# A vision tower on one core: first half's tokens in two column groups stored as plain rows, second half's stores cut by quarters, class value's products behind the first turnings

## The reference

```python
# 1. tokens: a state space kernel, 256 channels (two halves of 128), 64 complex states, 512 positions
dA = (1.0 + dtA / 2) / (1.0 - dtA / 2)
Ct = B[None] * C / (1.0 - dtA / 2) * dt[:, None]
V = jnp.exp(jnp.log(dA)[:, :, None] * l)
K = 2.0 * jnp.einsum('chn,hnl->chl', Ct, V).real
# 2. attention with 16 heads over layernorm(h); h also holds the class token
h = h + attn(layernorm(h))
# 3. 8 experts, two a token, over layernorm(h), then an output matrix
h = h + ffn(layernorm(h))
```

## Time and profile before

| | |
|---|---|
| median of 3 runs | 845.4 us (845.2 to 845.91) |
| the profiled execution | 845.3 us, span 843.5 us |
| granted TensorE clock, mean | 0.923 |
| PE busy | 706.9 us (84%) |
| DVE busy | 539.1 us (64%) |
| ACT busy | 405.1 us (48%) |
| POOL busy | 157.2 us (19%) |

### The profile page before, as it was taken

The page is one execution under the profiler, slowest core; times in us unless marked ns, Lnnn a source line. Parts: engine busy times, 40 slices in busy tenths (PEclk is TensorE's granted clock), DMA queues, the critical chain, the costliest instruction groups (busy, mean ns, idle before and its releaser), DMA issues.

```text
span 843.5 us, 17103 instructions
## 1 busy us (share of the span) xinstructions
PE 706.9 (84%) x5926; PEld 568.2 (67%) x5927; DVE 539.1 (64%) x1206; ACT 405.1 (48%) x1055; POOL 157.2 (19%) x282
## 2 busy tenths in 40 slices
PE   3898587667999999999999999786139999992998
PEld 2777487556868787777868686455137888882776
DVE  7959584356768676786768675636984444442665
ACT  3575254247667566675657575514343333331111
POOL 4000000010011111101111110121432223223451
PEclk9589999689999999999999999989558999996999
DMA  6100252320001010000000018124154656646674
GB/s 211 54 1 2 88 119 73 101 64 2 1 14 38 0 50 0 25 25 25 25 12 37 1 50 300 39 75 168 44 187 127 172 153 171 162 151 203 203 206 147
DMA packets 53082, 74.30 MB, mean 88 GB/s; under 512 B 24089, under 2 KB 26393, under 8 KB 52914
## 3 DMA queue, kind: packets, MB, share of 16 engines
q1 hardware_dynamic: 41362, 43.87, 15.9%
q0 software_dynamic: 5920, 19.40, 9.5%
q10 hardware_dynamic: 5760, 10.49, 3.2%
HBM read 45.42 MB, written 28.33 MB: 87 GB/s over the span
## 4 chain that ended last, share of the span: by engine, by line
PE 64%; DVE 17%; DMA 8%; ACT 4%; issue 4%; POOL 2%; SPq 1%; POOLq 0%; DVEq 0%; ACTq 0%
PE ps L1752 40%; PE ps L1840 7%; PE ps L1850 4%; DMA rows<-y_slots,slot_of 4%; PE ps L1833 3%; PE ps L2000 3%; DMA tok_dram<-so 3%; DVE ring L1243 2%; DVE ring L1244 2%; PE ps L1882 2%; DVE negmax L1304 2%; ACT prb L918 1%; DVE ew_lo L1599 1%; POOL rows L774 1%; PE ps L1696 1%
## 5 line engine op out<-in xcount | busy, mean ns | idle before, releaser
L926 ACT ACTIVATE pts<-ps 128x512 f32<-128x512 f32 x128 | 77.2, 603 | 120.3 <-PE ps L1840 120.3
L918 ACT ACTIVATE prb<-ps,negmax 128x257 f32<-128x257 f32 x256 | 117.9, 479 | 4.7 <-DVE negmax L1304 3.8
L1304 DVE TENSOR_REDUCE negmax<-ps 128x2 f32<-128x514 f32 x128 | 82.5, 687 | 35.1 <-PE ps L1833 35.1
L1840 PE MATMUL ps<-ident,prb 128*128 128x128 f32 x512 | 84.1, 288 | 9.3 <-DVE prb L1313 5.5
L1840 PEld LDWEIGHTS ps<-ident,prb 128*128 128x128 f32 x512 | 57.0, 143 | 34.3 <-issue 12.8
L1313 DVE TENSOR_SCALAR prb<-prb,rrec 128x258 f32<-128x258 f32 x256 | 73.5, 352 | 2.3
L1752 PE MATMUL ps<-ew_hi,xnT_hi 128*128 x160 | 66.9, 418 | 1.0 <-DVE xnT_lo L1489 1.0
L1050 ACT ACTIVATE rows<-ps 128x512 f32<-128x512 f32 x40 | 23.9, 598 | 87.5 <-DVE ps L1612 87.5
L1752 PE MATMUL ps<-ew_lo,xnT_hi 128*128 x160 | 63.5, 397 | 0.0
L1752 PE MATMUL ps<-ew_hi,xnT_lo 128*128 x160 | 63.5, 397 | 0.0
L1696 PE MATMUL ps<-ident,ring 128*128 128x128 f32 x384 | 47.8, 281 | 11.8 <-ACT rT L854 6.5
(11 more groups left out here) (372 smaller groups left out, 1872.7 us busy)
## 6 DMA issues: line engine op xcount, KB each, us to landing
y_slots<-rows ACTq DMA_DIRECT2D x40, 256.0 KB, 3.4
ew<-in_L_ffn_expert_w_dram SPq DMA_DIRECT2D x8, 1024.0 KB, 8.6
h_dram<-h_ob SPq DMA_DIRECT2D x17, 256.0 KB, 2.0
xn_dram<-tok SPq DMA_DIRECT2D x17, 256.0 KB, 2.2
tok_dram<-so SPq DMA_DIRECT2D x8, 512.0 KB
tok<-tok_dram SPq DMA_DIRECT2D x16, 256.0 KB, 4.4
h_early<-h_dram SPq DMA_DIRECT2D x9, 256.0 KB, 7.4
out_dram<-h_early SPq DMA_DIRECT2D x9, 256.0 KB
```

Source lines behind the costliest of these rows:

```text
L918: e = act.activation(prb[:, u % 2, j, 0:KEYS], ps[:, j, 0:KEYS], ACT.Exp, bias=negmax[:, u % 2, j:j + 1], accum_out=rowsum[:, u % 2, j:j + 1])
L926: act.activation(pts[:, slot:slot + 2, :, st * P:(st + 1) * P], ps[:, 4, :].rearrange("p (h t s) -> p h t s", h=2, t=HALVES), ACT.Copy).th ...
L1304: dve.tensor_reduce(negmax[:, u % 2, 2 * b:2 * b + 2], ps[:, 2 * b:2 * b + 2, 0:KEYS], AX_X, ALU.max, negate=True).then_inc(s["dve_max"], 1)
L1840: mm = pe.transpose(ps[:, 4, (2 * j + tt) * P:(2 * j + tt + 1) * P], prb[:, u % 2, 2 * b + j, tt * P:(tt + 1) * P], ident[:, :])
```

## The change

**Start-up.** The loads of rotations and spirals go ahead of Wv's, the biases ahead of Wo's. All four matrices are now turned one after the other; the class value's 48 products come behind all of them and use bank 5; what follows from them lies between turnings of pieces: `u`'s 13 products stand behind the fourth piece, in bank 4.

**First half.** `tokens_of_half` takes all 64 columns of `lT` (8 batches) at once, in two column groups of 64. A step's buffer is then 128 rows of 16 channels, and goes to `tok0_dram` as 128 plain rows of 4 KB. Each tile is loaded back by two DMAs of 64 channels. PE waits for the whole half's tables before the first product.

**Second half.** Products as before; each store is cut into four DMAs of 32 rows, two issued by SP and two by ACT.

```diff
-        tok_dram = nc.dram_tensor("tok_dram", [HALVES, NB * NA, P, NBP], F32).ap()
+        tok0_dram = nc.dram_tensor("tok0_dram", [P, P // 2, NBP], F32).ap()
+        tok1_dram = nc.dram_tensor("tok1_dram", [NB * NA, P, NBP], F32).ap()
...
+        def store_rows(engine, n, q):
+
+            first, at = (n // 2 - 2) * GROUP * NA, q * 32 + n % 2 * HB
+            engine.dma_start(tok1_dram[first:first + GROUP * NA, at:at + HB, :],
+                             so[q * 32:(q + 1) * 32, n % 2, :].rearrange("r (h b) -> r h b", h=HB)).then_inc(s_row[n % 2], 16)
...
-            sp.dma_start(wv_raw[:, :, :], Wv.rearrange("(o p) i -> p o i", p=P)).then_inc(s["loaded_wv"], 16)
-            sp.dma_start(rcol[:, 0, :], rot.rearrange("(k p) -> p k", p=P)).then_inc(s["loaded_vectors"], 16)
+            sp.dma_start(rcol[:, 0, :], rot.rearrange("(k p) -> p k", p=P)).then_inc(s["loaded_angles"], 16)
...
-            def store_group(g):
-                hf, first = g // 2, g % 2 * GROUP * NA
-                for k in range(2):
-                    n = 2 * g + k
-                    sp.wait_ge(s["act_tokens_kept"], n + 1)
-                    sp.dma_start(
-                        tok_dram[hf, first:first + GROUP * NA].rearrange("r (q i) b -> q r i b", q=4)[:, :, k * HB:(k + 1) * HB, :],
-                        so[:, n % 2, :].rearrange("p (i b) -> p i b", i=HB)).then_inc(s_row[n % 2], 16)
...
+                if hf == 0:
+                    for q in range(2):
+                        sp.dma_start(tok[q * 64:(q + 1) * 64, c, :].rearrange("h (a b) -> h a b", a=NA),
+                                     tok0_dram[q * 64 + c * NA:q * 64 + (c + 1) * NA, :, :].rearrange("a h b -> h a b")
+                                     ).then_inc(s[done], 16)
...
+            for n in range(4):
+                sp.wait_ge(s["act_tokens_kept"], n + 1)
+                sp.dma_start(tok0_dram[:, n * HB:(n + 1) * HB, :], so[:, n % 2, :].rearrange("r (h b) -> r h b", h=HB)
+                             ).then_inc(s_row[n % 2], 16)
...
             for g in range(2, 4):
-                store_group(g)
+                for n in (2 * g, 2 * g + 1):
+                    sp.wait_ge(s["act_tokens_kept"], n + 1)
+                    for q in range(2):
+                        store_rows(sp, n, q)
                 for row in s_row:
-                    sp.wait_ge(row, 16 * (g + 1))
+                    sp.wait_ge(row, 16 * (2 + 4 * (g - 1)))
...
                     e.then_inc(s["act_tokens_kept"], 1)
+                    if g >= 2:
+                        act.wait_ge(s["act_tokens_kept"], n + 1)
+                        for q in range(2, 4):
+                            store_rows(act, n, q)
 
             upper = PIECES - NB
+            value_high()
             for q in range(LOW_TURNS):
                 turned(q, rT, 4 * q)
-            w_high(3, wkT_hi)
-            keep_pieces(0, 0, 2)
-            w_low(3, wkT_lo)
-            keep_pieces(0, 2, PIECES)
+            value_low()
+            keep_pieces(0, 0, 4)
+            keep_u()
+            keep_pieces(0, 4, PIECES)
...
+            def tokens_of_half():
+                pe.wait_ge(s["act_table_kept"], TURNS)
+                for n in range(4):
+                    if n >= 2:
+                        pe.wait_ge(s["act_tokens_kept"], n - 1)
+                    for i in range(HB):
+                        for q in range(2):
+                            h = q * 64 + n * HB + i
+                            mm = pe.matmul(ps[q * 64:(q + 1) * 64, 4 + 2 * (n % 2) + i // 8, (i % 8) * NBP:(i % 8 + 1) * NBP],
+                                           lT[:, h, :], rT[:, h, :],
+                                           start=(i % 8 == 0), stop=(i % 8 == 7), skip_group_check=True)
+                    mm.then_inc(s["pe_tokens"], 1)
...
             pe.wait_ge(s["act_cls_x"], 2)
+            pe.wait_ge(s["act_w_low"], 4 * KC)
             for ci in range(KC):
...
-            pe.wait_ge(s["act_w_scaled"], KC)
-            w_turn(wq_raw, 2)
-            pe.wait_ge(s["act_cls_value"], 1)
-            less_high(ps[:, 1, 0:2 * KC], vc_hi[:, :, :].rearrange("p k t -> p (k t)")).then_inc(s["pe_cls_value"], 1)
-            w_rest(wqT_hi, 2)
+            turn_low(0)
+            pe.wait_ge(s["act_cls_value"], 3)
+            less_high(ps[:, 5, 0:2 * KC], vc_hi[:, :, :].rearrange("p k t -> p (k t)")).then_inc(s["pe_cls_value"], 1)
+            turn_pieces(0, 0, 4)
...
+            turn_pieces(0, 4, PIECES)
             pe.wait_ge(s["act_u"], 1)
-
-            turn_low(0)
-            pe.wait_ge(s["act_w_scaled"], 2 * KC)
-            w_turn(wk_raw, 3)
-            turn_pieces(0, 0, 2)
-            w_rest(wkT_hi, 3)
-            turn_pieces(0, 2, PIECES)
-            pe.wait_ge(s["act_w_low"], 4 * KC)
-            tokens(0)
-            tokens(1)
```

More of the change, by code:

```diff
@@ L669, in _ @@
             for row in s_row:
[L670 removed]
+                pool.wait_ge(row, 16 * 10)
             pool.memset(ones[:, :, :], 1.0).then_inc(s["pool_filled"], 1)
@@ L850, in _, with value_high, value_low, keep_u @@
             w_scale(wk_raw, k_scale)
+            w_low(2, wqT_lo)
+            act.activation(bvc_hi[:, :], bv_col[:, :], ACT.Copy).then_inc(s["act_cls_value"], 1)
+            w_high(3, wkT_hi)
+            w_low(3, wkT_lo)
+            act.wait_ge(s["act_cls_value"], 1)
+            act.activation(bvc_neg[:, :], bvc_hi[:, :].bitcast(F32), ACT.Copy, scale=-1.0).then_inc(s["act_cls_value"], 1)
+            value = ps[:, 5, 0:2 * KC].rearrange("p (k t) -> p k t", k=KC)
+            def value_high():
+                act.wait_ge(s["pe_cls_value"], 1)
+                act.activation(vc_hi[:, :, :], value, ACT.Copy).then_inc(s["act_cls_value"], 1)
+                act.wait_ge(s["pool_head_mask"], 1)
+                act.wait_ge(s["act_cls_value"], 3)
+                for ci in range(KC):
+                    act.activation(vblk_hi[:, ci, :], mask[:, ci, :], ACT.Copy, scale=vc_hi[:, ci, 0:1].bitcast(F32)
+                                   ).then_inc(s["act_vblk"], 1)
+            def value_low():
+                act.wait_ge(s["pe_cls_value"], 2)
+                act.activation(vc_lo[:, :, :], value, ACT.Copy).then_inc(s["act_cls_value"], 1)
+                act.wait_ge(s["act_cls_value"], 4)
+                for ci in range(KC):
+                    act.activation(vblk_lo[:, ci, :], mask[:, ci, :], ACT.Copy, scale=vc_lo[:, ci, 0:1]
+                                   ).then_inc(s["act_vblk"], 1)
+                act.wait_ge(s["act_vblk"], 2 * KC)
+                act.activation(vblk_hi[:, :, NHEAD:NHEAD + 1], bvc_hi[:, :].bitcast(F32).unsqueeze(2), ACT.Copy
+                               ).then_inc(s["act_vblk"], 1)
+                for ci in range(KC):
+                    act.activation(vblk_lo[:, ci, NHEAD:NHEAD + 1], bv_col[:, ci:ci + 1], ACT.Identity,
+                                   bias=bvc_neg[:, ci:ci + 1]).then_inc(s["act_vblk"], 1)
+            def keep_u():
+                for k in range(SEL):
+                    act.wait_ge(st_h[k], 16)
+                act.wait_ge(s["pe_u"], 1)
+                act.activation(u_sb[0:32, :], ps[0:32, 4, :], ACT.Copy).then_inc(s["act_u"], 1)
             def turned(n, dst, col):
@@ L910, in _ @@
             for row in s_row:
-                act.wait_ge(row, 16 * CHUNKS // 2)
+                act.wait_ge(row, 16 * 10)
             def exp_unit(c, u):
```

87 lines of the change are left out of this document (34 added, 53 removed).

## The result

The changed kernel takes 842.79 us (median of 17 runs, 839.03 to 849.84) against 845.33 us of the kernel before (17 runs, 843.74 to 848.66): ratio 0.9964, 95% interval 0.9947 to 0.9982. It is faster by 2.5 us (3.0 by the ratio), a fifth of the 12.8 that were forecast, and the time lies above the range of 824 to 839. The profiled execution has a span of 839.5 us, 4.0 shorter.

A forecast was written before the change was run, and what follows sets the result against it. Bound: a chain of PE's class products, DVE's pieces and two token stores of about 12 us using 0.27 of the DMA engines. 845.3 + 3.5 - 10.3 - 4.9 - 1.1 = 832.5 us, range 824 to 839.

The forecast's parts named there:

- Part 3: Second half's end: shorter stores let loads and norm finish earlier, so q and k products start at 153.5, -4.9 us.
- part 1: Start-up: class products behind the weights and `u` between pieces cost +3.5 us at the first half's last turning.
- the gain in clock: q and k products: PE idles less in front, so half of a possible 2.2 us at full clock is won, -1.1.
- Part 2: First half's tokens: shorter steps and stores over more DMA engines let DVE go on at 98.5 instead of 108.81, -10.3 us.
- Rivals B and C: First half: B (10%): two groups of 64 columns don't overlap, 838.7 us. C (10%): stores stay slow, 835 to 837 us.
- The signs: Changed profile, first half's tokens: no ACT wait for a store over 2 us, DMA share near 1 in short stretches.
- the slack in part 3: Second half's end: the loads path has 3.5 us to spare, so slower quarters cost nothing until they take 7 us.
- The price put on ACT's issues: Second half: ACT issuing two DMAs behind each buffer costs 0.9 us in all, with its own wait.
- Its second term: Start-up: `u`'s products and bias between pieces make DVE stand about 3.6 us in front of piece 6.
- Its first term: Start-up: DVE restarts about where it does now, the wait passing from `u` to the class products; taken as 0.
- rival A: Start-up: the class products run at full clock, about 5.3 us instead of 10.03; time 825.7 us; chance 25%.
- Rival D: Second half: SP's 16 loads block its stores; at 2.5 us per load the time would be 850 us; chance 3%.

The follow-up runs named there:

- quarters by SP: The kernel before with only the change's token part, the norm ahead of DVE's cast, and all four second-half store quarters issued by SP; ratio 0.9794.
- stores and norm: The kernel before with only the change's token part (start-up as before) and the first norm ahead of DVE's cast; 829.6 us, ratio 0.9805.

## Why the prediction was wrong

The forecast was 832.5 us; measured were 842.8. Part 3 had the mechanism wrong, part 1 a landing too early, and the gain in clock rested on part 3.

- **Part 2 (-10.3): right, and by its mechanism.** A to B is 10.75 shorter (9.2 to 11.0 over the nine kernels with both column groups and 128 rows). Stores took 3.25 in the chain (assumed 3.4; 4.45 to 4.77 in three kernels), a step of two column groups 1.92 (assumed 2.0), with no pause. Rivals B and C did not occur. The signs held: ACT waits 1.09 and 1.18 us for a store, and the DMA share is near 1 in short stretches. Two readings were off without harm: the pauses named "issue" do not stand between steps (in the kernel before too they come after 208, 335 and 463 of 512 instructions), and the slack in part 3, below.
- **Part 3 (-4.9): wrong, the largest error.** The step that failed is "the normed tiles are there at 146: they now wait for PE, not the reverse". It followed the data (store, load, norm) and not DVE's program, in which the cast waits for ACT ahead of the norm. Measured +0.28. With the cast behind the norm the same part is worth -5.70 (B to C 25.62 after 31.32), 0.8 more than forecast since PE's turning then runs at full clock (1.09 instead of 1.94), so the rest of the reckoning was sound. The slack of the loads path was forecast at 3.5 and is 2.3 there (`xhat` done at 139.57, PE ready at 141.90). The price put on ACT's issues, 0.9 behind each buffer, was right as well, and avoidable: 1.0 to 1.6 us of B to C.
- **Part 1 (+3.5): the sign right, the size too small, +5.87 measured.** Its second term, 3.6 for `u` between pieces, measured 3.31 (DVE's restart to A, 32.67 after 29.36). Its first term, no change of DVE's restart, was off by 2.56 (58.37 after 55.81). The step that failed is "it lands near 12": Wv's load took 8.5 us behind the loads of rotations and spirals instead of 5.6, and landed at 14.3. The products at half clock (10.15) and `turn_low` (3.54) took what was assumed, and rival A did not occur: the window 42.70 to 52.80 has

```profile
42.70:52.80 10.10, 10.10 (x49) 10.10 (x50) 3.81 (x4) 0.00 (x0) 0.00 (x0) 0.51 0.01 2
```

- **Clock in q and k (-1.1): nothing, +0.25.** It rested on part 3: PE's idle time in front was to fall from 6.6 to 3 and stayed 6.13 us. The first 4.96 us of q and k stand at 0.50 in the changed kernel; over the kernels with the norm ahead of the cast in the changed or token-only form q and k took 13.27 to 13.29 us (11.76 once), over the others 13.28 to 14.32. So about half a us may come with the mend (one kernel without it has 13.28 as well), where -1.1 had been booked.
- **Rival D** did not occur; SP issued the 16 loads from 113.21 on within 10.85 us and was at the second half's stores in time. Its price was added up wrong: with loads of 2.5 us SP is 24 us late, 20.5 of it beyond the slack, which gives 853, not 850.

In sum +5.87 - 10.75 + 0.28 + 0.25, and 0.3 in the 670 us behind, make the span's -4.0, against +3.5 - 10.3 - 4.9 - 1.1. The token part with the norm ahead, 829.6 us and with quarters by SP 828.7 (medians), lies in the range that was forecast for the whole change.

## What to carry to other kernels

When a long wait is about to go, read each engine's program in order from there, not only the chain of data: list what stands ahead of the next step on its own engine and what each of those waits for. A wait that ends 2 us before the one you remove stands in no chain and takes over at once. The timeline does list it: look there for long waits off the chain (10.32 us of DVE here).

Look at a DMA's outermost dimension first: a store with one of 4 ran four times as long as one with 128. Cutting the same store into quarters on the same engine, with the norm's place mended, had nearly the whole gain without a new layout (0.9801 beside 0.9794).

Work moved between two steps of a pipeline whose bound has no slack costs nearly its full length (3.3 of 3.8 us here), even when it was on the path where it stood before.

## What the runs showed of the hardware

- A 1 MB load issued behind five small loads of single words took 8.5 us, ahead of them 5.5 and 5.6 (8.3 to 8.6 over four kernels with it behind, 5.2 to 5.9 over ten with it ahead; which of the small ones holds it was not tried).
- The same start-up code ran its 48 class products in 8.12 to 10.03 us over eight executions, and A moved over 3.4 us, for the most part with them (82.2 to 82.4 with products under 8.8 us, 83.7 to 85.6 with longer ones). The window 24.30 to 32.30 of the kernel with stores and norm has a granted clock of 0.62, the same stretch with quarters by SP 0.50, both with PE busy throughout:

```profile
24.30:32.30 8.00, 8.00 (x48) 8.00 (x47) 7.62 (x23) 3.81 (x7) 0.00 (x0) 0.62 0.10 25
```

```profile
24.60:34.60 10.00, 10.00 (x48) 10.00 (x49) 9.62 (x25) 3.50 (x7) 0.00 (x0) 0.50 0.03 5
```

  A single profile of such a stretch is uncertain by 2 us, more than many edits are worth.
- The store that the chain waits for took 3.17 to 3.73 us in six executions with 128 outer rows and 4.45 to 4.77 in three, with A to B at 31.0 to 31.2 and at 32.4 to 32.7. What sets it was not found.
- PE's pause named "issue" in the last tokens step was 1.18 to 2.41 us over the fourteen executions, all with the same code there. Its cause stays open.
